# One-hots of an adjacency build, made chunk by chunk with per-partition scalars instead of in batches of eight chunks

## The chip, the cores and the metric

One core of one Trainium2 chip. The metric is the device time of one execution in microseconds (us). The kernel before takes 494.15 us, the median of three runs (493.7 to 494.18).

## The reference

One graph-transformer layer over N = 1250 nodes of width 512, with a graph of 21250 directed edges (`src`, `dst`, one weight each). The part that matters here is the graph part:

```python
m = jnp.maximum(jnp.max(weighting_gate), 0.0)
exp_e = jnp.exp(weighting_gate - m)
row_sum = jax.ops.segment_sum(exp_e, src, num_segments=n_nodes)
atten_e = exp_e / (row_sum[src] + 1e-06)
Mfeat = source_features @ Wm + bm
out0 = jax.ops.segment_sum(atten_e[:, None] * Mfeat[dst], src, num_segments=n_nodes)
out1 = jax.ops.segment_sum(atten_e[:, None] * Mfeat[src], dst, num_segments=n_nodes)
```

Around it stand a layer norm, a linear attention (`mix`) whose result is added, and at the end a mixture of eight experts on the sum.

## The kernel before

The kernel writes out, by hand, one instruction stream for each engine, with semaphores between them. The two segment sums are done as matrix products with a dense adjacency `adj` (1250 x 1250, kept as 10 row tiles of 125 nodes by 5 windows of 250 columns, so 50 buckets). `adj` is built in three steps.

First the edges are sorted into buckets of (row tile, column window), each bucket padded to whole chunks of 128 edges: NCH = 216 chunks, taken as PAIRS = 108 pairs of two. GpSimd scatters most edges into a DRAM table `slots`; the last 54 columns of edges are placed by matmuls with one-hots instead (line 702, semaphore `sort_ps`). VectorE then adds the two parts (lines 1248 and 1250) into `keys` (row and column of each edge within its tile and window) and `parts` (the edge weight as two f16 parts, WT = 2).

Second, the adjacency build. For each chunk, TensorE multiplies a weighted row one-hot (`s_hot`, 128 edges by CH = 128 rows, once for each of the two weight parts) with a column one-hot (`d_hot`, 128 edges by AW = 251 columns; the last column is 1 and gives row sums). That is four matmuls for a pair (line 739), all f16, which add into one of four PSUM banks; a one-column matmul (line 731) resets ahead of each pair. ScalarE copies two windows (502 columns) out to `adj` after each pair (line 1646, `win_ok`). The reset of pair p waits for `win_ok` of p - 2. The banks and columns to use are data: TensorE loads them into registers, the 16 of `in_at` at every pair with p % 8 = 0 and the 8 of `new_at` at every pair with p % 8 = 4 (`read_in`, `read_new`).

The one-hots come from VectorE, in 28 batches: 26 of four pairs (eight chunks), then two of two pairs. A batch of four is three instructions: `s_one`, the plain row one-hots of eight chunks (line 1264); `d_hot`, the column one-hots (line 1268); and `s_hot`, the row one-hots times both weight parts (line 1276). All are two-operand f16 instructions on a table of column numbers that stores each number twice (`col_2`), so that the two chunks of a pair lie interleaved, element by element. `d_hot` and `s_hot` are rings of DB = 4 batches. TensorE waits for `batch_ok` once for each batch, VectorE for `chunk_ps` before it overwrites a ring entry. Before its first pair TensorE runs RUN_UP = 10 matmuls that nobody reads (line 708).

Third, once all 108 copies are done (`win_ok`), VectorE sums rows (line 1287), and TensorE turns `adj` (line 751) and multiplies with it (lines 758 and on). The update, the router and the experts follow in order.

Of the kernel before, what the change touches and what calls it, by code (L numbers as in the profile page):

```python
# [11 lines left out]
F16 = mybir.dt.float16  # L12
F32R = mybir.dt.float32r
ALU = mybir.AluOpType
# [11 lines left out]
CH = 128  # L26
# [8 lines left out]
WIN = 250  # L35
NW = N // WIN
AW = WIN + 1
# [4 lines left out]
NCH = (NE + NB * (CH - 1)) // CH + 1  # L42
# [8 lines left out]
WT = 2  # L51
E_UP, E_LEAST, E_ANY = 2.0 ** 15, 2.0 ** -24, 2.0 ** 100
PB, DB = 4, 4
# [44 lines left out]
BATCHES = [(i, i + PB) for i in range(0, PAIRS - PB, PB)] + [(PAIRS - PB, PAIRS - 2), (PAIRS - 2, PAIRS)]  # L98
# [13 lines left out]
def build(nc, x, edge_src, edge_dst, edge_w, consts, halves, biases, small, fold, wqkv, wp, bvt, w1f, w2f, b2f, out):  # L112
    with ExitStack() as ctx:
# [3 lines left out]
        def sem(name):  # L117
            return ctx.enter_context(nc.semaphore(name))
# [19 lines left out]
        def half(name):  # L138
            a, w = HALVES[name]
            return hlf[:, a:a + w]  # L140
# [15 lines left out]
        def place(name, col, shape, dt=F32):  # L156
            return nc.alloc_sbuf_tensor_at(name, shape, dt, offset=base + 4 * col)
# [56 lines left out]
        keys = place("keys", 33728, [128, 2, NCH], F16)  # L214
        parts = place("parts", 33944, [128, PAIRS // PB, WT, 2 * PB], F16)
        d_hot = place("d_hot", 16064, [128, DB, PB, AW, 2], F16)
        s_one = place("s_one", 20088, [128, 2, PB, CH, 2], F16)
        s_hot = place("s_hot", 21112, [128, DB, WT, PB, CH, 2], F16)
# [106 lines left out]
        def piece(a, i):  # L325
# [45 lines left out]
        key_ok, sort_hot, sort_ps, part_ok, col_ok, one_ok, batch_ok, chunk_ps, win_ok = (  # L371
            sem("key_ok"), sem("sort_hot"), sem("sort_ps"), sem("part_ok"), sem("col_ok"), sem("one_ok"),
            sem("batch_ok"), sem("chunk_ps"), sem("win_ok"))
# [25 lines left out]

        def batch_of(pair):  # L400

            n = next(i for i, (a, b) in enumerate(BATCHES) if a <= pair < b)
            return n, pair - BATCHES[n][0]

# [121 lines left out]
        def _(pe):  # L526
# [195 lines left out]
            for p in range(PAIRS):  # L722
# [10 lines left out]
                n, q = batch_of(p)  # L733
                if p == BATCHES[n][0]:
                    pe.wait_ge(batch_ok, n + 1)
                for j in range(2):
                    at_in = pe.snap(in_at[(2 * p + j) % BATCH], min_val=512 * WB0, max_val=512 * (WB0 + WBANKS - 1) + AW)
                    for i in range(WT):
                        mm = pe.matmul(flat_banks[:, bass.ds(at_in, AW)], s_hot[:, n % DB, i, q, :, j],  # L739
                                       d_hot[:, n % DB, q, :, j], start=False, stop=(i == WT - 1), skip_group_check=True)  # L740
# [191 lines left out]
        def _(dve):  # L932
# [309 lines left out]
            for n in range(EARLY + 1, PCOLS // 2):  # L1242
                sort_late(n)
            dve.wait_ge(sort_ps, PCOLS // 2)
            dve.memset(d_hot[:, :, :, WIN, :], 1.0)
# [4 lines left out]
            dve.tensor_tensor(parts[:, :, :, :].rearrange("p n i m -> p i n m"),  # L1250
                              got_h[:, :, 2:4].rearrange("p (n m) k -> p k n m", m=2 * PB),
                              bank[0][:, 0:2 * NCH].rearrange("p (k n m) -> p k n m", k=2, m=2 * PB),
                              ALU.add).then_inc(part_ok, 1)
            dve.wait_ge(part_ok, 1)
            dve.wait_ge(col_ok, 1)
            for n, (p0, p1) in enumerate(BATCHES):
                k, r = p1 - p0, n % DB

                def of_keys(i):
                    return keys[:, i, 2 * p0:2 * p1].rearrange("p (a j) -> p a j", j=2).unsqueeze(2)  # L1260

                if n >= 2:
                    dve.wait_ge(batch_ok, n - 1)
                dve.tensor_tensor(s_one[:, n % 2, 0:k, :, :], col_2[:, 0:CH, :].unsqueeze(1).to_broadcast([128, k, CH, 2]),
                                  of_keys(0).to_broadcast([128, k, CH, 2]), ALU.is_equal).then_inc(one_ok, 1)
                if n >= DB:
                    dve.wait_ge(chunk_ps, BATCHES[n - DB][1])
                dve.tensor_tensor(d_hot[:, r, 0:k, 0:WIN, :], col_2[:, :, :].unsqueeze(1).to_broadcast([128, k, WIN, 2]),  # L1268
                                  of_keys(1).to_broadcast([128, k, WIN, 2]), ALU.is_equal)
                if n == 0:  # L1270
                    dve.wait_ge(part_ok, 2)
                dve.wait_ge(one_ok, n + 1)
                both = parts[:, p0 // PB, :, :].rearrange("p i (a j) -> p i a j", j=2)
                if k == PB:
                    shape = [128, WT, PB, CH, 2]
                    last = dve.tensor_tensor(s_hot[:, r, :, :, :, :], s_one[:, n % 2, :, :, :].unsqueeze(1).to_broadcast(shape),  # L1276
                                             both.unsqueeze(3).to_broadcast(shape), ALU.mult)
                else:
                    a = p0 % PB
                    for i in range(WT):  # L1280
                        last = dve.tensor_tensor(s_hot[:, r, i, 0:k, :, :], s_one[:, n % 2, 0:k, :, :],
                                                 both[:, i, a:a + k, :].unsqueeze(2).to_broadcast([128, k, CH, 2]), ALU.mult)
                last.then_inc(batch_ok, 1)
# [576 lines left out]
```

## Time and profile before

| | |
|---|---|
| median of 3 runs | 494.15 us (493.7 to 494.18) |
| profiled execution, its own time | 493.5 us |
| its span, from the first to the last instruction | 491.4 us |
| adjacency build, first pair's matmul to last copy | 231.5 to 312.5 us |
| VectorE busy, adjacency build, batches | 228.4 to 305.8 us |
| granted TensorE clock, mean | 0.959 |

```profile
## 2 busy tenths in 40 slices
PE   3665999999999999999777777899898957999992
DVE  6786688877786888698999998478279874455552
ACT  4577999988897123363777777554335662666550
PEclk9878999999999999999999999999999858999998
```

Each digit is one fortieth of the span, about 12.3 us, and gives the busy share in tenths. PE is TensorE's matmuls, DVE VectorE, ACT ScalarE; PEclk is the TensorE clock granted, in tenths of full. The adjacency build is the 19th to 25th digit. Start times below are in us from the start of the span, and a duration is an instruction's own, which for VectorE overlaps a little with the next one's.

### The profile page before, as it was taken

How to read it: one execution, taken by the hardware profiler on the slowest of the kernel's cores; microseconds unless marked ns; L12 is line 12 of the kernel's file. 1: busy time of each engine (PE TensorE's matmuls, PEld its weight loads, DVE VectorE, ACT ScalarE, POOL GpSimd, SP SyncE). 2: the span in 40 equal slices, each digit the busy share in tenths (PEclk: the TensorE clock that was granted, in tenths of full speed). 3: DMA queues.
4: the chain of work that ended last, by engine and by line, in shares of the span. 5: the costliest groups of instructions: out<-in, count | busy, mean ns of one | idle time of the engine just before them, and what ended most of it. 6: DMA issues, size and time to landing. Idle time of an engine off the chain costs nothing.

```text
span 491.4 us, 8811 instructions
## 1 busy us (share of the span) xinstructions
PE 424.5 (86%) x2701; PEld 343.4 (70%) x2701; DVE 366.9 (75%) x717; ACT 298.3 (61%) x845; POOL 194.8 (40%) x160
## 2 busy tenths in 40 slices
PE   3665999999999999999777777899898957999992
PEld 1454887888887788877555555799876746788881
DVE  6786688877786888698999998478279874455552
ACT  4577999988897123363777777554335662666550
POOL 0378878688887787870000000000000008254321
PEclk9878999999999999999999999999999858999998
DMA  7992000000000000005000000000006964243210
GB/s 228 284 250 49 1 3 3 1 4 2 3 3 1 2 2 3 2 3 191 2 1 2 1 2 0 3 1 0 1 1 258 412 225 128 74 120 110 68 65 16
DMA packets 15742, 31.07 MB, mean 63 GB/s; under 512 B 7652, under 2 KB 8283, under 8 KB 14675
## 3 DMA queue, kind: packets, MB, share of 16 engines
q1 hardware_dynamic: 9266, 23.21, 14.6%
q0 software_dynamic: 6432, 7.31, 7.5%
q8 instruction: 24, 0.39, 0.3%
q14 instruction: 20, 0.16, 0.1%
HBM read 24.90 MB, written 7.37 MB: 66 GB/s over the span
## 4 chain that ended last, share of the span: by engine, by line
PE 64%; ACT 14%; DVE 10%; issue 6%; DMA 3%; POOL 1%; SPq 1%; ACTq 0%; DVEq 0%; POOLq 0%
PE banks L569 25%; PE banks L739 9%; PE banks L892 7%; PE banks L758 4%; ACT adj L1646 4%; PE banks L751 2%; ACT q_sb L1580 2%; PE banks L824 2%; PE banks L650 2%; PE banks L883 2%; ACT k_sb L1580 1%; DVE chunk_1h L1214 1%; DMA x_rows<-factors 1%; ACT q_sb L1563 1%; PE banks L731 1%
## 5 line engine op out<-in xcount | busy, mean ns | idle before, releaser
L496 POOL DMA_INDIRECT slots<-record,row_i x116 | 153.7, 1325 | 40.7 <-issue 40.7
L507 POOL DMA_INDIRECT rec<-x_rows,get_i x17 | 18.7, 1098 | 190.7 <-DMA x_rows<-factors 185.8
L1646 ACT ACTIVATE adj<-banks x108 | 58.4, 588 | 27.9 <-PE banks L739 26.8
L569 PE MATMUL banks<-w_hi,xT_hi 128*125 128x512 f32 (+1 forms) x160 | 61.5, 385 | 5.7 <-DVE xT_lo L1085 5.7
L739 PE MATMUL banks<-d_hot,s_hot 128*128 128x251 f16 x432 | 60.0, 276 | 0.2
L569 PE MATMUL banks<-w_lo,xT_hi 128*125 128x512 f32 (+1 forms) x160 | 60.1, 375 | 0.0
L569 PE MATMUL banks<-w_hi,xT_lo 128*125 128x512 f32 (+1 forms) x160 | 60.0, 375 | 0.0
L569 PEld LDWEIGHTS banks<-w_hi,xT_hi 128*125 128x125 f32 x160 | 30.9, 193 | 12.0 <-issue 6.1
L739 PEld LDWEIGHTS banks<-d_hot,s_hot 128*128 128x128 f16 x432 | 33.5, 98 | 7.5 <-issue 0.7
L569 PEld LDWEIGHTS banks<-w_lo,xT_hi 128*125 128x125 f32 x160 | 30.9, 193 | 5.8
L569 PEld LDWEIGHTS banks<-w_hi,xT_lo 128*125 128x125 f32 x160 | 30.6, 191 | 6.1
L516 POOL DMA_INDIRECT out<-o_sb,out_i x17 | 17.1, 1005 | 40.9 <-DVE o_sb L1462 40.9
L1268 DVE TENSOR_TENSOR d_hot<-col,keys 128x2000 f16<-128x2000 f16 (+1 forms) x28 | 32.3, 1153 | 0.0
L731 PE MATMUL banks<-hlf 128*128 128x1 f16 x108 | 18.3, 170 | 16.1 <-ACT adj L1646 16.1
L1276 DVE TENSOR_TENSOR s_hot<-s_one,parts 128x2048 f16<-128x2048 f16 x26 | 31.6, 1215 | 0.0
L1457 DVE TENSOR_TENSOR y_sb<-banks,b_sb 128x512 f32<-128x512 f32 x17 | 11.8, 691 | 26.2 <-PE banks L569 26.2
L731 PEld LDWEIGHTS banks<-hlf 128*128 128x128 f16 x108 | 10.4, 96 | 28.9 <-issue 26.9
L1580 ACT ACTIVATE q_sb<-q_sb,hmax 125x64 f32<-125x64 f32 x80 | 26.7, 335 | 4.3 <-DVE hmax L1113 4.2
L1609 ACT ACTIVATE row_1h<-row_one,sort_f 125x128 f16<-125x128 f16 x54 | 19.7, 432 | 13.8 <-DVE row_one L1208 8.0
L1580 ACT ACTIVATE k_sb<-k_sb,hmax 125x64 f32<-125x64 f32 x80 | 26.6, 333 | 0.0
L702 PE MATMUL banks<-chunk_1h,row_1h 125*128 125x216 f16 x216 | 22.8, 258 | 3.2 <-DVE chunk_1h L1214 2.2
L1617 ACT ACTIVATE xT_hi<-banks 128x500 fp32r<-128x500 f32 x10 | 5.9, 588 | 30.6 <-PE banks L663 30.6
(297 smaller groups left out, 1083.1 us busy)
## 6 DMA issues: line engine op xcount, KB each, us to landing
w_raw<-in_w2f SPq DMA_DIRECT2D x4, 1024.0 KB, 8.1
w_raw<-in_wqkv SPq DMA_DIRECT2D x3, 1024.0 KB, 15.2
x_rows<-rec SPq DMA_DIRECT2D x10, 224.0 KB
w1a<-in_w1f SPq DMA_DIRECT2D x1, 2048.0 KB, 7.8
w1b<-in_w1f SPq DMA_DIRECT2D x1, 2048.0 KB, 16.5
b_sb<-in_b2f SPq DMA_DIRECT2D x1, 2048.0 KB, 22.9
slots<-record,row_i POOLq DMA_INDIRECT x116, 2.6
rec<-in_x SPq DMA_DIRECT2D x1, 1120.0 KB
```

The costliest lines, as they stand in the source:

```text
L496: pool.indirect_dma_start(slots, bass.IndirectOffsetOnAxis(ap=row_i[:, c:c + 1], axis=0), record[:, c, :], None).then_inc(slot_st, 16)
L569: mm = pe.matmul(dst, ab, cd, start=(i == 0), stop=(i == n - 1))
L702: mm = pe.matmul(bank[1 - v // 2][:, v % 2 * NCH:(v % 2 + 1) * NCH], row_1h[:, n % RS, v, :, j], chunk_1h[:, n % RS, :, j], start=(n == 0 ...
L731: pe.matmul(flat_banks[:, bass.ds(at_new, 1)], before, zero_col, start=True, stop=False, skip_group_check=True)
L739: mm = pe.matmul(flat_banks[:, bass.ds(at_in, AW)], s_hot[:, n % DB, i, q, :, j], d_hot[:, n % DB, q, :, j], start=False, stop=(i == WT - ...
L758: mm = pe.matmul(hid_at(w), msg[:, t, GH:MD], adjw[:, t, w, 0:WIN], start=(t == 0), stop=(t == NT - 1), skip_group_check=True)
L892: mm = pe.matmul(bank[1][:, 0:F], xsT[:, c % 2, k, :], w1_sb[k // 2][:, k % 2, bass.ds(e * F, F)], start=(k == 0), stop=(k == KD - 1))
L1268: dve.tensor_tensor(d_hot[:, r, 0:k, 0:WIN, :], col_2[:, :, :].unsqueeze(1).to_broadcast([128, k, WIN, 2]), of_keys(1).to_broadcast([128, ...
L1276: last = dve.tensor_tensor(s_hot[:, r, :, :, :, :], s_one[:, n % 2, :, :, :].unsqueeze(1).to_broadcast(shape), both.unsqueeze(3).to_broadc ...
L1580: last = act.activation(ah, ah, ACT.Exp, bias=hmax[:, i, h:h + 1], accum_out=hsum[:, i, h:h + 1])
L1609: last = act.activation(row_1h[:, n % RS, VD, :, j], row_one[:, n % 2, :, j], ACT.Copy, scale=sort_f[:, 2 * n + j:2 * n + j + 1])
L1646: act.activation(adj[:, bass.ds(w, BW2)], flat_banks[0:TP, bass.ds(out_at, BW2)], ACT.Copy).then_inc(win_ok, 1)
```

## The change

`keys` and `parts` become f32, one column for each chunk. The table `col_2`, the intermediate `s_one` and the batches are no longer used in this stage. For each chunk VectorE now issues three `tensor_scalar` instructions: one compares the table of 250 column numbers with that chunk's column key, given as a per-partition scalar, and writes `d_hot`; two compare the 128 row numbers with the row key and multiply by one weight part, both as per-partition scalars, and write one part of `s_hot` each. The two chunks of a pair lie one after the other instead of interleaved. The rings hold RING_P = 16 pairs. TensorE waits once for each pair (`hot_pair`), and VectorE waits for `chunk_ps` pair by pair from the 17th on. The matmuls, the resets, the copies and the register loads stay.

```diff
--- before.py
+++ after.py
@@ -50,7 +50,8 @@
 HB = BATCH // 2
 WT = 2
 E_UP, E_LEAST, E_ANY = 2.0 ** 15, 2.0 ** -24, 2.0 ** 100
-PB, DB = 4, 4
+RING_P = 16
+DW = AW + 1
 WB0, WBANKS, IDLE_IN, IDLE_OUT = 2, 4, 6, 7
 TRASH, SPARE = NB * AW, 4
 BW2 = 2 * AW
@@ -95,7 +96,6 @@
 
 
 PAIRS = NCH // 2
-BATCHES = [(i, i + PB) for i in range(0, PAIRS - PB, PB)] + [(PAIRS - PB, PAIRS - 2), (PAIRS - 2, PAIRS)]
 LOTS = [(i * LC, min(i * LC + LC, EC)) for i in range(NL)]
 MARKED = (3, 6, 8, 9)
 
@@ -211,11 +211,11 @@
         row_1h = place("row_1h", 16584, [TP, RS, VT, CH, 2], F16)
         got = place("got", 32216, [128, NCH, RW])
         got_h = got[:, :, :].bitcast(F16)
-        keys = place("keys", 33728, [128, 2, NCH], F16)
-        parts = place("parts", 33944, [128, PAIRS // PB, WT, 2 * PB], F16)
-        d_hot = place("d_hot", 16064, [128, DB, PB, AW, 2], F16)
-        s_one = place("s_one", 20088, [128, 2, PB, CH, 2], F16)
-        s_hot = place("s_hot", 21112, [128, DB, WT, PB, CH, 2], F16)
+        keys = place("keys", 33728, [128, 2, NCH])
+        parts = place("parts", 34160, [128, WT, NCH])
+        d_hot = place("d_hot", 16064, [128, RING_P, 2, DW], F16)
+        s_hot = place("s_hot", 21112, [128, RING_P, WT, 2, CH], F16)
+
 
 
         hidc = place("hidc", 26064, [128, 2, WIN])
@@ -368,9 +368,9 @@
             sem("num_ps"), sem("num_used"), sem("ao_ok"), sem("aoT_ps"), sem("aoT_ok"), sem("mix_ps"), sem("mix_ok"))
 
         sort_one, sort_act = sem("sort_one"), sem("sort_act")
-        key_ok, sort_hot, sort_ps, part_ok, col_ok, one_ok, batch_ok, chunk_ps, win_ok = (
-            sem("key_ok"), sem("sort_hot"), sem("sort_ps"), sem("part_ok"), sem("col_ok"), sem("one_ok"),
-            sem("batch_ok"), sem("chunk_ps"), sem("win_ok"))
+        key_ok, sort_hot, sort_ps, part_ok, col_ok, hot_pair, chunk_ps, win_ok = (
+            sem("key_ok"), sem("sort_hot"), sem("sort_ps"), sem("part_ok"), sem("col_ok"),
+            sem("hot_pair"), sem("chunk_ps"), sem("win_ok"))
         rinv_ok, in_ok, in_ps, turn_ps, turn_a, turn_v, out_split = (
             sem("rinv_ok"), sem("in_ok"), sem("in_ps"), sem("turn_ps"), sem("turn_a"), sem("turn_v"),
             sem("out_split"))
@@ -396,11 +396,6 @@
 
             for a, b in ((0, 112), (112, TP)):
                 eng.dma_start(dst(a, b), srcs(a, b)).then_inc(s, 16)
-
-        def batch_of(pair):
-
-            n = next(i for i, (a, b) in enumerate(BATCHES) if a <= pair < b)
-            return n, pair - BATCHES[n][0]
 
         def ctx_copies(copy, h):
 
@@ -730,14 +725,12 @@
                     pe.wait_ge(win_ok, p - 2)
                 pe.matmul(flat_banks[:, bass.ds(at_new, 1)], before, zero_col, start=True, stop=False,
                           skip_group_check=True)
-                n, q = batch_of(p)
-                if p == BATCHES[n][0]:
-                    pe.wait_ge(batch_ok, n + 1)
+                pe.wait_ge(hot_pair, p + 1)
                 for j in range(2):
                     at_in = pe.snap(in_at[(2 * p + j) % BATCH], min_val=512 * WB0, max_val=512 * (WB0 + WBANKS - 1) + AW)
                     for i in range(WT):
-                        mm = pe.matmul(flat_banks[:, bass.ds(at_in, AW)], s_hot[:, n % DB, i, q, :, j],
-                                       d_hot[:, n % DB, q, :, j], start=False, stop=(i == WT - 1), skip_group_check=True)
+                        mm = pe.matmul(flat_banks[:, bass.ds(at_in, AW)], s_hot[:, p % RING_P, i, j, :],
+                                       d_hot[:, p % RING_P, j, 0:AW], start=False, stop=(i == WT - 1), skip_group_check=True)
                 mm.then_inc(chunk_ps, 1)
 
 
@@ -1242,45 +1235,25 @@
             for n in range(EARLY + 1, PCOLS // 2):
                 sort_late(n)
             dve.wait_ge(sort_ps, PCOLS // 2)
-            dve.memset(d_hot[:, :, :, WIN, :], 1.0)
+            dve.memset(d_hot[:, :, :, WIN:DW], 1.0)
 
             dve.wait_ge(ld_got, 16)
             dve.tensor_tensor(keys[:, :, :], got_h[:, :, 0:2].rearrange("p c k -> p k c"),
                               bank[1][:, 0:2 * NCH].rearrange("p (k c) -> p k c", k=2), ALU.add).then_inc(part_ok, 1)
-            dve.tensor_tensor(parts[:, :, :, :].rearrange("p n i m -> p i n m"),
-                              got_h[:, :, 2:4].rearrange("p (n m) k -> p k n m", m=2 * PB),
-                              bank[0][:, 0:2 * NCH].rearrange("p (k n m) -> p k n m", k=2, m=2 * PB),
-                              ALU.add).then_inc(part_ok, 1)
-            dve.wait_ge(part_ok, 1)
-            dve.wait_ge(col_ok, 1)
-            for n, (p0, p1) in enumerate(BATCHES):
-                k, r = p1 - p0, n % DB
-
-                def of_keys(i):
-                    return keys[:, i, 2 * p0:2 * p1].rearrange("p (a j) -> p a j", j=2).unsqueeze(2)
-
-                if n >= 2:
-                    dve.wait_ge(batch_ok, n - 1)
-                dve.tensor_tensor(s_one[:, n % 2, 0:k, :, :], col_2[:, 0:CH, :].unsqueeze(1).to_broadcast([128, k, CH, 2]),
-                                  of_keys(0).to_broadcast([128, k, CH, 2]), ALU.is_equal).then_inc(one_ok, 1)
-                if n >= DB:
-                    dve.wait_ge(chunk_ps, BATCHES[n - DB][1])
-                dve.tensor_tensor(d_hot[:, r, 0:k, 0:WIN, :], col_2[:, :, :].unsqueeze(1).to_broadcast([128, k, WIN, 2]),
-                                  of_keys(1).to_broadcast([128, k, WIN, 2]), ALU.is_equal)
-                if n == 0:
-                    dve.wait_ge(part_ok, 2)
-                dve.wait_ge(one_ok, n + 1)
-                both = parts[:, p0 // PB, :, :].rearrange("p i (a j) -> p i a j", j=2)
-                if k == PB:
-                    shape = [128, WT, PB, CH, 2]
-                    last = dve.tensor_tensor(s_hot[:, r, :, :, :, :], s_one[:, n % 2, :, :, :].unsqueeze(1).to_broadcast(shape),
-                                             both.unsqueeze(3).to_broadcast(shape), ALU.mult)
-                else:
-                    a = p0 % PB
+            dve.tensor_tensor(parts[:, :, :], got_h[:, :, 2:4].rearrange("p c k -> p k c"),
+                              bank[0][:, 0:2 * NCH].rearrange("p (k c) -> p k c", k=2), ALU.add).then_inc(part_ok, 1)
+            dve.wait_ge(part_ok, 2)
+            places = half("cols")
+            for p in range(PAIRS):
+                if p >= RING_P:
+                    dve.wait_ge(chunk_ps, p - RING_P + 1)
+                for j in range(2):
+                    c = 2 * p + j
+                    dve.tensor_scalar(d_hot[:, p % RING_P, j, 0:WIN], places, keys[:, 1, c:c + 1], None, ALU.is_equal)
                     for i in range(WT):
-                        last = dve.tensor_tensor(s_hot[:, r, i, 0:k, :, :], s_one[:, n % 2, 0:k, :, :],
-                                                 both[:, i, a:a + k, :].unsqueeze(2).to_broadcast([128, k, CH, 2]), ALU.mult)
-                last.then_inc(batch_ok, 1)
+                        last = dve.tensor_scalar(s_hot[:, p % RING_P, i, j, :], places[:, 0:CH], keys[:, 0, c:c + 1],
+                                                 parts[:, i, c:c + 1], ALU.is_equal, ALU.mult)
+                last.then_inc(hot_pair, 1)
 
 
             dve.wait_ge(win_ok, PAIRS)
```

## Rows read from the trace of the kernel before

**Rows 1.** The chain that ended last, 225 to 314 us: its share by line

```profile
by line: PE banks L739 51.6%; ACT adj L1646 22.8%; issue 9.1%; PE banks L731 5.9%; PE banks L708 4.8%; ACTq L1646 1.6%; PE banks L751 1.5%; PE banks L702 1.1%; DVE chunk_1h L1214 0.8%; DVE row_1h L1212 0.6%; PE banks L758 0.3%; DVE row_one 
```

**Rows 2.** Busy time by stretch: us, each engine's busy time (instructions), clock, DMA

```profile
core 0: us, PE busy (x) PEld busy (x) DVE busy (x) ACT busy (x) POOL busy (x), PEclk, DMA share, GB/s
...
271.00:281.00 10.00, 7.84 (x70) 5.45 (x68) 10.00 (x12) 6.95 (x13) 0.00 (x0) 1.00 0.00 0
301.00:312.00 11.00, 9.08 (x79) 6.12 (x76) 4.76 (x10) 8.19 (x16) 0.00 (x0) 1.00 0.01 1
...
409.00:413.20 4.20, 1.99 (x11) 1.29 (x10) 1.49 (x1) 2.11 (x3) 3.29 (x4) 0.99 0.45 131
413.20:416.60 3.40, 3.40 (x11) 2.63 (x10) 0.08 (x1) 0.00 (x0) 2.51 (x3) 0.51 0.70 187
```

**Rows 3.** Order of time, 268 to 277 us: start, duration, engine, line, idle before

```profile
268.31 0.68 DVE L1264 TENSOR_TENSOR s_one<-col,keys 128x1024 f16<-128x1024 f16 x1
...
268.91 1.19 DVE L1268 TENSOR_TENSOR d_hot<-col,keys 128x2000 f16<-128x2000 f16 x1
...
270.02 1.22 DVE L1276 TENSOR_TENSOR s_hot<-s_one,parts 128x2048 f16<-128x2048 f16 x1
...
270.38 0.17 PE L731 MATMUL banks<-hlf 128*128 128x1 f16 x1 [0.37 <-ACT adj L1646]
...
271.16 0.68 DVE L1264 TENSOR_TENSOR s_one<-col,keys 128x1024 f16<-128x1024 f16 x1
...
273.65 0.17 PE L731 MATMUL banks<-hlf 128*128 128x1 f16 x1 [0.91 <-ACT adj L1646]
...
276.38 0.17 PE L731 MATMUL banks<-hlf 128*128 128x1 f16 x1 [0.36 <-ACT adj L1646]
```

**Rows 4.** Who waited for whom, 228 to 313 us

```profile
ACT adj L1646 <- PE banks L739: 26.8, 28, 6.1
PE banks L731 <- ACT adj L1646: 16.1, 26, 1.0
```

**Rows 5.** Order of time around the start and the end of the build

```profile
227.20 4.39 PE L708 MATMUL banks<-cst 128*128 128x250 f32 x20
...
228.44 0.68 DVE L1264 TENSOR_TENSOR s_one<-col,keys 128x1024 f16<-128x1024 f16 x1
...
305.01 0.75 DVE L1281 TENSOR_TENSOR s_hot<-s_one,parts 128x512 f16<-128x512 f16 x2
...
311.12 0.63 PE L739 MATMUL banks<-d_hot,s_hot 128*128 128x251 f16 x4
312.51 0.24 DVE L1287 TENSOR_REDUCE rs<-adj 125x10 f32<-125x50 f32 x1 [6.75 <-ACT adj L1646]
```

**Rows 6.** Groups on VectorE by shape: busy us, mean ns of one

```profile
L1462 DVE SCALAR_TENSOR_TENSOR o_sb<-y_sb,rec 128x512 f32<-128x512 f32 x17 | 12.8, 752 | 0.6
...
L1457 DVE TENSOR_TENSOR y_sb<-banks,b_sb 128x512 f32<-128x512 f32 x17 | 11.8, 691 | 26.2 <-PE banks L569 26.2
```

**Rows 7.** Order of time on VectorE, instructions with and without per-partition scalars

```profile
3.77 0.25 DVE L943 TENSOR_SCALAR s_hi<-src_i 125x170 int32<-125x170 int32 x1 [3.77 <-DMA dst_i<-in_edge_dst]
3.93 0.24 DVE L944 TENSOR_SCALAR d_hi<-dst_i 125x170 int32<-125x170 int32 x1
...
73.22 0.14 DVE L1073 TENSOR_SCALAR of_c<-of_b 125x1 f32<-125x1 f32 x1
73.28 0.20 DVE L1074 TENSOR_SCALAR of_c<-of_b,cst 125x1 f32<-125x1 f32 x1
...
358.95 0.60 DVE L1343 TENSOR_SCALAR hid<-comb,mv,rstd 125x128 f32<-125x128 f32 x2
...
362.39 0.61 DVE L1323 TENSOR_SCALAR comb<-banks,rinv 125x128 f32<-125x128 f32 x2 [1.64 <-PE banks L794]
```

**Rows 8.** Lines 1323 and 1343: durations min/median/max, ns

```profile
L1323 DVE TENSOR_SCALAR comb<-banks,rinv x10: 339/342/351, 350.8 to 376.2; 125x128 f32<-125x128 f32 x10
...
L1343 DVE TENSOR_SCALAR hid<-comb,mv,rstd x10: 339/344/348, 353.2 to 379.6; 125x128 f32<-125x128 f32 x10
```


## Prediction

> **What bounds the kernel now.** I read the chain that ended last first, cut to the adjacency build and its edges. The reader is to see that VectorE is all but absent from it: 51.6% lies on the four matmuls of a pair (line 739), 22.8% on ScalarE's copies (line 1646), 9.1% on issue [rows 1]. Then busy time by stretch: in the middle of the build VectorE is busy 10.00 us of 10, TensorE 7.84, ScalarE 6.95, and after the batches end VectorE falls to 4.76 of 11 [rows 2]. So there are two loops of nearly the same pace. The order of time gives both. VectorE starts a batch of four pairs at 268.31 and the next at 271.16: 2.85 us, 0.71 us a pair. TensorE starts the reset of a group at 270.38, the next at 273.65, the third at 276.38: 6.00 us for eight pairs, 0.75 us a pair [rows 3]. In the list of waits nobody waits for VectorE: ScalarE waits 26.8 us for line 739 and TensorE 16.1 us for the copies [rows 4]. TensorE's loop (matmuls, copies, register loads) sets the pace, and VectorE runs ahead: its last batch is done at 305.76, while the last pair's matmuls start at 311.12 and the row sum that opens the next stage at 312.51, 6.75 us after VectorE went idle [rows 5]. VectorE has 0.04 us a pair to spare, and 5.4 us at the end. Whatever makes its pair dearer than 0.75 us moves the end of the stage.
>
> **Part 1: what goes.** Per four pairs, `s_one` takes 0.60 us from its start to the next instruction's, `d_hot` 1.11 and `s_hot` 1.14 [rows 3]. These give the law for a two-operand f16 instruction: 1024 elements 0.60 us, 2048 elements 1.14 us, so 0.53 ns an element, two elements per 1.05 ns, and about 0.06 us fixed. Instructions of this size pay the fixed part three times in four pairs. It hardly counts.
>
> **Part 2: what comes.** Per pair, two `tensor_scalar` of 250 elements with one per-partition scalar and four of 128 elements with two, six instructions in place of 0.75. In all 648 instructions in place of 86. Each has three prices: the fixed part, a charge for the scalar, and the elements by a rate.
>
> The fixed part without such a scalar: line 943, 170 int32 elements with a constant, starts 0.16 us before line 944 [rows 7]. With two elements per 1.05 ns that is 0.09 + 0.07. I take 0.065 us.
>
> The charge for the scalar: line 1074 has one element and a per-partition scalar and takes 0.20 us, line 1073 the same with a constant 0.14 [rows 7]. Line 1462, 512 elements with one such scalar, takes 752 ns where line 1457 without takes 691 [rows 6]. Both give 0.06 us.
>
> Whether it hides when such instructions follow each other: line 1323 (PSUM source, 128 elements, one scalar) does two in 0.61 us, one taking 342 ns, so they start 0.27 us apart; 0.065 + 0.134 + 0.06 = 0.26 [rows 7, 8]. It doesn't hide. Line 1343 (SBUF source, two scalars, a subtraction and a multiplication, the very form of the new `s_hot`, in f32) does two in 0.60 us, one taking 344 ns: 0.26 us apart [rows 7, 8]. That row can be read in two ways. A: one charge whatever the number of scalars, and one element per 1.05 ns (0.065 + 0.134 + 0.06 = 0.26). B: a charge for each scalar, and two elements per tick (0.065 + 0.067 + 0.12 = 0.25).
>
> For f16 no row has a `tensor_scalar`. Under A the engine keeps one operand path, and f16 packing gives two elements a tick as in rows 3: `d_hot` 0.065 + 0.131 + 0.06 = 0.256, `s_hot` 0.065 + 0.067 + 0.06 = 0.192, a pair 0.512 + 0.768 = 1.28 us. Under B f16 doubles f32's rate to four a tick: `d_hot` 0.191, `s_hot` 0.219, a pair 0.382 + 0.876 = 1.26 us. The two come out alike, so I need not choose. I take 1.28, the end that lies with the slightly dearer measured spacing. The bounds from the nearest rows: below, no charge and four a tick, 2 x 0.131 + 4 x 0.099 = 0.66 us; above, f16 treated as line 1343 under A, one element a tick, 2 x 0.387 + 4 x 0.259 = 1.81 us.
>
> The Trainium skill, "VectorE: DVE Perf Modes", section on the TRN2 errata, puts a VectorE instruction on SBUF at 58 cycles of 0.96 GHz plus the elements over the mode's factor, and its tier table lets `tensor_scalar` on 16-bit data run at 4x. By it the pair would be an estimated 0.63 us, cheaper than now. The same section warns that the fixed cost is paid per instruction and advises 512 elements or more, which speaks against this change; and its formula has no term for the scalar, which rows 6 and 7 show at 0.06 us.
>
> **Part 3: the waits.** TensorE waits for each pair instead of each fourth; behind that wait stand its four matmuls, and behind those ScalarE's copy. The reset is ahead of it. Price: a wait that is met costs nothing that rows 3 show (between zero and 0.03 us a pair if VectorE is ahead); if VectorE is late it is VectorE's time, counted below. VectorE's new wait for `chunk_ps` looks 16 pairs back, as the ring of four batches did, and is met long before. The f32 sum for `keys` and `parts` is as large as now; VectorE's loop starts after both instead of after the first, at about 228.6 instead of 228.44 [rows 5], 0.1 to 0.2 us. That TensorE could have its first pair at 230 is worth nothing: its idle matmuls of line 708 run from 227.20 to 231.59 [rows 5]. Contiguous operands for the matmuls: zero; they run at 2.4 GHz by their columns already (clock 1.00 [rows 2]). The extra column of a ring row and the memset of 64 instead of 32 elements: below 0.05 us.
>
> **The sum.** VectorE: 228.6 + 108 x 1.28 = 366.8. Then the last pair: 0.1 us for the end of the last write and the signal, and from the start of its matmuls to the row sum 312.51 - 311.12 = 1.39 us [rows 5]. The row sum starts at 368.3 instead of 312.51: +55.8 us. What follows it doesn't depend on anything that runs beside the build, so it shifts as it is.
>
> **The clock.** TensorE would be busy 7.84 us of 13.3 pairs, 0.59 us a pair [rows 2], in 1.28 us: 46%. The stretch 409 to 413.2 has 1.99 of 4.20 us, 47%, and after it the clock reads 0.51, the 1.2 GHz level, for 3.4 us of dense work [rows 2]. So I expect a fall during the build. At half clock a pair is at most 1.17 us and with today's gaps (2.16 us in 13.3 pairs) at most 1.33, so at worst 0.05 us a pair more than VectorE's (+5 us); I expect none, since busy time counts a pipeline's fill that doesn't double. The next stage would start low: half of 3.4 us lost, 1.7, and 0.5 for the last pair: 2.2 us. Bounds 0 and 7.
>
> 493.5 (the profiled execution: span 491.4 and 2.1 around it) + 55.8 + 2.2 = 551.5. The median of the runs is 0.65 above the profiled one: 552.2.
>
> **Rivals.**
>
> *The scalars stop every fast mode.* Line 1343 under A, and f16 no better: 1.81 us a pair, 195.5 us, the row sum at 425.6, +113.1. With the clock's 2.2: 609. For it: one row, read one way. Against: rows 3 show f16 packing on the same engine.
>
> *One charge and four a tick.* 2 x 0.191 + 4 x 0.159 = 1.02 us, 109.9 us, +27.5: 524. It needs line 1343 to have been slowed by something that f16 escapes.
>
> *The charge hides in a long run, at two a tick.* 2 x 0.196 + 4 x 0.132 = 0.92 us, 99.4 us, +17: 513.
>
> *No charge at all, four a tick: the other side.* 0.66 us a pair is below TensorE's 0.75, so VectorE is hidden as now, and TensorE's loop of 6.00 us for eight pairs sets the end: 81 us from 231.5, what it takes now. 494, between 492.5 (waits of the first groups gone) and 496 (a wait for each pair). It decides below 0.75 us a pair. The skill's formula above is this rival. Lines 1323 and 1343, back to back and still 0.26 apart, speak against it.
>
> **How the numbers follow.** The forecast (1.24 to 1.34 us a pair, 546 to 562) 58%; every fast mode lost 13%; one charge at four a tick 12%; the charge hidden at two a tick 6%; no charge 9%; elsewhere between 2%. The point is 552. The range takes in the forecast, the dear rival and the case at 524, 83%: 522 to 612. A measurement of this kernel can tell 0.2%, 1 us, from no change. Of the 9% I give 3 to faster, 4 to same, 2 to slower; all else is slower: 0.93.
>
> **What would show it.** In the profile after: VectorE busy without a gap from 228.6 to about 367, `d_hot` durations near 0.34 us under A or 0.28 under B, `s_hot` near 0.28 or 0.30, with starts 0.06 to 0.08 us closer than durations; the idle time before line 739's matmuls put down to VectorE; no idle time before the row sum beyond some 1.5 us; the clock at 0.5 in the build and for some 3 us after. The prediction is wrong if the pair's starts are under 1.2 us apart, if the clock stays at 1.00 (then 2.2 us less), or if TensorE's pace at half clock exceeds VectorE's.

## The result and the profile after

The changed kernel takes 550.85 us (550.45 to 551.78, four runs) against 493.92 (492.47 to 494.18) before: a ratio of 1.116, 95% interval 1.113 to 1.119. Predicted were 552.0. The profiled execution has a span of 548.4 us, 57.0 more than before.

From the page after: the engines' busy times and the forty slices.

```profile
PE 469.9 (86%) x2701; PEld 360.1 (66%) x2701; DVE 428.1 (78%) x1279; ACT 303.5 (55%) x845; POOL 192.4 (35%) x160
...
PE   4485999999989999868888887879998885899992
...
PEclk9977999999999999965555555558999995999998
```

VectorE's busy time rose by 61 us (366.9 before), TensorE's by 45 (424.5 before) with the same 2701 matmuls. The clock reads 0.5 to 0.6 for ten slices in the middle, where it was full before. Who waited for whom in the build, and the chain's share by line from 225 to 371 us:

```profile
PE banks L732 <- DVE s_hot L1254: 19.0, 67, 0.7
...
by line: DVE s_hot L1254 65.6%; DVE d_hot L1252 29.3%; PE banks L744 1.5%; PE banks L732 0.7%; PE banks L697 0.7%; DVE chunk_1h L1207 0.5%; ACT adj L1619 0.4%; DVE row_1h L1205 0.4%; issue 0.4%; DVE parts L1243 0.4%; DVE keys L1241 0.3%; DV
```

Before, nobody waited for VectorE and the chain ran over TensorE and ScalarE [rows 1, 4]. Now two VectorE lines carry 95% of it. Order of time at the start and the end of the build, and the first use of line 1296 (line 1323 before), which I take as the mark behind the turning stage, in which TensorE turns `adj` and multiplies with it:

```profile
230.33 0.28 DVE L1252 TENSOR_SCALAR d_hot<-hlf,keys 128x250 f16<-128x250 f16 x1
230.53 0.53 DVE L1254 TENSOR_SCALAR s_hot<-hlf,keys,parts 128x128 f16<-128x128 f16 x2
230.97 0.28 DVE L1252 TENSOR_SCALAR d_hot<-hlf,keys 128x250 f16<-128x250 f16 x1
...
231.29 0.59 PE L732 MATMUL banks<-d_hot,s_hot 128*128 128x251 f16 x4
...
366.96 1.02 PE L732 MATMUL banks<-d_hot,s_hot 128*128 128x251 f16 x4 [0.26 <-DVE s_hot L1254]
...
368.74 0.24 DVE L1260 TENSOR_REDUCE rs<-adj 125x10 f32<-125x50 f32 x1 [1.92 <-ACT adj L1619]
...
368.85 2.43 PE L744 MATMUL banks<-cst,adj 125*125 125x125 f32 x10 [0.87 <-ACT adj L1619]
...
409.84 0.35 DVE L1296 TENSOR_SCALAR comb<-banks,rinv 125x128 f32<-125x128 f32 x1 [5.72 <-PE banks L787]
```

The same mark before:

```profile
350.77 0.35 DVE L1323 TENSOR_SCALAR comb<-banks,rinv 125x128 f32<-125x128 f32 x1 [5.72 <-PE banks L794]
```

`d_hot` starts 0.195 us before the next instruction; two `s_hot` together take 0.445, so 0.22 each; the next chunk starts 0.64 us later, a pair 1.28. The row sum starts at 368.74 instead of 312.51 [rows 5]: +56.2 us. TensorE's first pair still starts only after its idle matmuls, at 231.29, and the first turn of a tile takes 2.43 us.

Busy time by stretch, columns as in [rows 2]:

```profile
231.00:237.70 6.70, 4.05 (x35) 2.70 (x34) 6.70 (x33) 3.43 (x6) 0.00 (x0) 1.00 0.23 98
...
271.00:281.00 10.00, 8.39 (x40) 4.57 (x40) 10.00 (x48) 4.48 (x8) 0.00 (x0) 0.50 0.00 1
...
471.90:475.30 3.40, 2.53 (x14) 1.83 (x12) 0.42 (x1) 1.27 (x3) 2.50 (x3) 1.00 0.70 185
```

At full clock TensorE is busy 4.05 us of 6.70 (and 1.85 of the last 3.70), then the clock falls at 237.7 and stays at 0.50 until 374.3, in the turning stage. The busy time it then shows, 8.39 of 10, is the same four matmuls and reset a pair at 1.2 GHz: 1.07 us a pair instead of 0.59.

### The profile page after: what moved, and what is told of

It is laid out like the page before. It is cut to its first block, busy times and chain, and to the rows that moved or that the text cites. A ratio compares the mean times of both kernels' runs of the same rounds, so it can differ in the third digit from the quotient of the medians.

```text
span 548.4 us, 9371 instructions
## 1 busy us (share of the span) xinstructions
PE 469.9 (86%) x2701; PEld 360.1 (66%) x2701; DVE 428.1 (78%) x1279; ACT 303.5 (55%) x845; POOL 192.4 (35%) x160
## 4 chain that ended last, share of the span: by engine, by line
PE 49%; DVE 35%; ACT 9%; issue 4%; POOL 1%; SPq 0%; DMA 0%; DVEq 0%; ACTq 0%; POOLq 0%
PE banks L564 22%; DVE s_hot L1254 17%; DVE d_hot L1252 8%; PE banks L885 6%; PE banks L751 4%; PE banks L744 2%; ACT q_sb L1553 2%; PE banks L645 1%; PE banks L868 1%; PE banks L876 1%; ACT k_sb L1553 1%; DVE chunk_1h L1207 1%; PE banks L532 1%; ACT q_sb L1536 1%; DVE stat L1331 1%
## 5 line engine op out<-in xcount | busy, mean ns | idle before, releaser
L491 POOL DMA_INDIRECT slots<-record,row_i x116 | 151.5, 1306 | 40.7 <-issue 40.7
L732 PE MATMUL banks<-d_hot,s_hot 128*128 128x251 f16 x432 | 105.8, 401 | 20.3 <-DVE s_hot L1254 19.0
L1254 DVE TENSOR_SCALAR s_hot<-hlf,keys,parts 128x128 f16<-128x128 f16 x432 | 112.2, 297 | 0.0
L1619 ACT ACTIVATE adj<-banks x108 | 63.5, 589 | 79.2 <-PE banks L732 79.1
L732 PEld LDWEIGHTS banks<-d_hot,s_hot 128*128 128x128 f16 x432 | 45.6, 128 | 53.4 <-issue 40.0
L1252 DVE TENSOR_SCALAR d_hot<-hlf,keys 128x250 f16<-128x250 f16 x216 | 58.8, 272 | 0.0
L726 PEld LDWEIGHTS banks<-hlf 128*128 128x128 f16 x108 | 14.7, 136 | 22.8 <-issue 18.1
L726 PE MATMUL banks<-hlf 128*128 128x1 f16 x108 | 21.6, 200 | 6.4 <-issue 6.2
L751 PE MATMUL banks<-adj,msg 125*128 125x250 f32 x100 | 24.6, 396 | 0.0
```

The source lines that it names most:

```text
L491: pool.indirect_dma_start(slots, bass.IndirectOffsetOnAxis(ap=row_i[:, c:c + 1], axis=0), record[:, c, :], None).then_inc(slot_st, 16)
L726: pe.matmul(flat_banks[:, bass.ds(at_new, 1)], before, zero_col, start=True, stop=False, skip_group_check=True)
L732: mm = pe.matmul(flat_banks[:, bass.ds(at_in, AW)], s_hot[:, p % RING_P, i, j, :], d_hot[:, p % RING_P, j, 0:AW], start=False, stop=(i == ...
L751: mm = pe.matmul(hid_at(w), msg[:, t, GH:MD], adjw[:, t, w, 0:WIN], start=(t == 0), stop=(t == NT - 1), skip_group_check=True)
L1252: dve.tensor_scalar(d_hot[:, p % RING_P, j, 0:WIN], places, keys[:, 1, c:c + 1], None, ALU.is_equal)
L1254: last = dve.tensor_scalar(s_hot[:, p % RING_P, i, j, :], places[:, 0:CH], keys[:, 0, c:c + 1], parts[:, i, c:c + 1], ALU.is_equal, ALU.mult)
```

## Experiments

The theory on the pair's price: a fixed part of 0.065 us, 0.06 us for each per-partition scalar, not hidden in a long run of such instructions, and f16 elements at four per 1.05 ns. The rivals: one charge an instruction, a floor for short instructions, a charge for f32 scalars beside an f16 stream, and a slow rate. The first four runs build on the changed kernel. The diffs are shortened: `...` stands for what is left out, and small edits that only make room for them (a copy of the keys in f32, the layout of a ring) are told in words. Where one run is given and no range, the program ran once.

**One scalar instead of two.**

```diff
-                        ... keys[:, 0, c:c + 1], parts[:, i, c:c + 1], ALU.is_equal, ALU.mult)
+                        ... keys[:, 0, c:c + 1], 1.0, ALU.is_equal, ALU.mult)
```

> The changed kernel with the constant 1.0 in place of the weight part as second scalar of s_hot (it leaves the edge weights out of adj). Theory (each per-partition scalar costs 0.06 us, not hidden): s_hot spacing 0.225 to 0.165 us, d_hot unchanged at 0.195, a pair 1.28 to 1.04 us, the build 26 us shorter, about 525 us. Rival (one charge for an instruction, whatever the number of scalars; the rest of the 0.225 is the second ALU operation): no change, 551 us.

Measured 523.42 us (one run). Order of time on VectorE:

```profile
260.17 0.42 DVE L1254 TENSOR_SCALAR s_hot<-hlf,keys 128x128 f16<-128x128 f16 x2
260.50 0.29 DVE L1252 TENSOR_SCALAR d_hot<-hlf,keys 128x250 f16<-128x250 f16 x1
260.69 0.41 DVE L1254 TENSOR_SCALAR s_hot<-hlf,keys 128x128 f16<-128x128 f16 x2
```

Two `s_hot` take 0.33 us from the first's start to the next `d_hot`, 0.165 each, and `d_hot` 0.19. The pair is 1.04 us. The second ALU operation is still there, the second scalar isn't: the charge is for each scalar. This row also sets the rate: with one scalar each, 250 columns cost 0.19 and 128 cost 0.165, some 0.03 us for 122 columns, which is four per 1.05 ns (0.032) and not two (0.064). (`s_hot` still has one ALU operation more than `d_hot`; were that dear, the columns would be cheaper still.)

**No per-partition scalar.**

```diff
-  dve.tensor_scalar(d_hot[...], places, keys[:, 1, c:c + 1], None, ALU.is_equal)
+  dve.tensor_scalar(d_hot[...], places, float(c), None, ALU.is_equal)
-  dve.tensor_scalar(s_hot[...], places[:, 0:CH], keys[:, 0, c:c + 1], parts[:, i, c:c + 1], ALU.is_equal, ALU.mult)
+  dve.tensor_scalar(s_hot[...], places[:, 0:CH], float(c % CH), 1.0, ALU.is_equal, ALU.mult)
```

> The changed kernel with constants in place of all per-partition scalars (it leaves keys and weights out, so adj holds other numbers). Theory (fixed part 0.065 us, four elements per 1.05 ns): d_hot spacing 0.131 us, s_hot 0.099, a pair 0.66 us, below TensorE's loop of 0.75 us, so the time is again the kernel before's, 493 to 496 us. Rival (short f16 instructions have a floor of about 0.19 us each whatever their scalars): a pair 1.15 us or more, 535 us or more.

Measured 495.79 us. Order of time on VectorE, and its row sum:

```profile
260.14 0.29 DVE L1254 TENSOR_SCALAR s_hot<-hlf 128x128 f16<-128x128 f16 x2
260.35 0.22 DVE L1252 TENSOR_SCALAR d_hot<-hlf 128x250 f16<-128x250 f16 x1
260.48 0.29 DVE L1254 TENSOR_SCALAR s_hot<-hlf 128x128 f16<-128x128 f16 x2
...
312.88 0.24 DVE L1260 TENSOR_REDUCE rs<-adj 125x10 f32<-125x50 f32 x1 [10.22 <-ACT adj L1619]
```

0.105 and 0.13 us, a chunk 0.34, a pair 0.68: below TensorE's 0.75, and the row sum is back at 312.88. The same 648 instructions, the same waits for each pair and the same layout move the row sum by 0.4 us once VectorE is under TensorE's pace. The loss of 56 us there is in the scalars: 0.30 of the 0.64 us a chunk.

**f16 scalars.** `keys` and `parts` are kept as F16.

> The changed kernel with keys and parts kept as f16, so that the per-partition scalars are f16 instead of f32. Theory (the charge is a fixed latency of fetching the scalar, and f32 scalars don't hold the fast mode back): spacing 0.195 and 0.225 us as in the changed kernel, 551 us. Rival (the charge is the f32 scalar beside an f16 stream): the spacing falls to some 0.13 and 0.10 us, towards 494 us.

Measured 551.08 us.

```profile
260.05 0.29 DVE L1252 TENSOR_SCALAR d_hot<-hlf,keys 128x250 f16<-128x250 f16 x1
260.25 0.54 DVE L1254 TENSOR_SCALAR s_hot<-hlf,keys,parts 128x128 f16<-128x128 f16 x2
260.69 0.29 DVE L1252 TENSOR_SCALAR d_hot<-hlf,keys 128x250 f16<-128x250 f16 x1
```

0.20 and 0.22 us, as in the changed kernel. The scalar's type doesn't matter. Durations of `s_hot` read 0.31 here where the changed kernel showed 0.30, at the same spacing: between profiles only the spacing may be compared.

**TensorE kept busy.** The clock theory: its fall comes from TensorE's own idle time in the build.

```diff
                     pe.matmul(flat_banks[:, bass.ds(at_new, 1)], before, zero_col, ...)
+                if p >= 4:
+                    for _ in range(3):
+                        pe.matmul(bank[IDLE_IN][:, 0:WIN], before, half("cols"), start=True, stop=True)
                 pe.wait_ge(hot_pair, p + 1)
```

> The changed kernel, plus three matmuls of 250 columns that nobody reads, ahead of TensorE's wait for each pair from the fifth on. Theory (the clock fell in the build because TensorE waits for VectorE's one-hots there; cost 3.2 us: 0.4 in the last pair, 2.8 in the next stage): clock 1.00 through the build, VectorE's pair unchanged at 1.28 us, row sum at about 368.3, first use of line 1296 about 3.2 us earlier, 547.6 us in all. Rival (the clock follows something else, such as VectorE's use of SBUF): the clock falls all the same, seven matmuls a pair at half clock take about 1.6 us and TensorE becomes the bound, some 580 us.

Measured 550.46 us (547.66 to 552.07, four runs), ratio to before 1.117 (1.110 to 1.124). Order of time at the end of the build, the first use of line 1299 (1296 in the changed kernel), and the stretch 251 to 301:

```profile
365.74 0.60 PE L735 MATMUL banks<-d_hot,s_hot 128*128 128x251 f16 x4 [0.33 <-DVE s_hot L1257]
...
367.10 0.24 DVE L1263 TENSOR_REDUCE rs<-adj 125x10 f32<-125x50 f32 x1 [1.50 <-ACT adj L1622]
...
405.37 0.61 DVE L1299 TENSOR_SCALAR comb<-banks,rinv 125x128 f32<-125x128 f32 x2 [5.72 <-PE banks L790]
...
251.00:301.00 50.00, 35.88 (x310) 23.75 (x309) 50.00 (x236) 23.05 (x40) 0.00 (x0) 1.00 0.01 2
```

The clock stays at 1.00, with TensorE busy 35.88 us of 50, and VectorE gets through as many instructions (236) in these 50 us as in the changed kernel. From the last pair's matmuls to the row sum it takes 1.36 us, in the changed kernel 1.78; from the row sum to line 1299 38.27, there 41.10, and before 38.26. So the fall costs 0.4 and 2.8 us as the theory said, and filling TensorE's idle time takes it away. The total doesn't show it beyond the spread: what comes after that line takes 140.9 us here and 138.6 in the changed kernel's profile. The clock there reads 0.78, 0.50 and 0.53 in the three stretches of 10 us that begin 30 us after that line, and 1.00, 0.50 and 0.65 in the changed kernel; that this is the whole of the 2.3 us is not shown. That part of the expectation, 547.6 us, came out only in the fastest run.

The next two do one part of the change alone, on the kernel before.

**`d_hot` alone by chunk.** The ring keeps its four batches, now with the two chunks of a pair one after the other; the keys are copied to f32 once.

```diff
-  dve.tensor_tensor(d_hot[:, r, 0:k, 0:WIN, :], col_2..., of_keys(1)..., ALU.is_equal)
+  for c in range(2 * p0, 2 * p1):
+      dve.tensor_scalar(d_hot[:, r, c // 2 - p0, c % 2, 0:WIN], half("cols"), keys_f[:, c:c + 1], None, ALU.is_equal)
```

> The kernel before with the d_hot part of the change alone: 216 instructions of 250 columns with one f32 per-partition scalar, in a ring of four batches as before; s_one and s_hot stay in batches. Theory: a batch 0.60 + 8 x 0.195 + 1.14 = 3.30 us instead of 2.85, 0.825 us a pair, just above TensorE's 0.75, so VectorE bounds the build: row sum at about 320.2 instead of 312.5, 501 us. Rival (single instructions of this size cost more among large ones, or less): the d_hot spacing is not 0.195 us.

Measured 503.26 us.

```profile
264.62 0.69 DVE L1267 TENSOR_TENSOR s_one<-col,keys 128x1024 f16<-128x1024 f16 x1
265.22 1.65 DVE L1273 TENSOR_SCALAR d_hot<-hlf,keys_f 128x250 f16<-128x250 f16 x8
266.78 1.23 DVE L1280 TENSOR_TENSOR s_hot<-s_one,parts 128x2048 f16<-128x2048 f16 x1
267.91 0.70 DVE L1267 TENSOR_TENSOR s_one<-col,keys 128x1024 f16<-128x1024 f16 x1
...
320.01 0.24 DVE L1291 TENSOR_REDUCE rs<-adj 125x10 f32<-125x50 f32 x1 [2.28 <-ACT adj L1650]
```

A batch is 3.29 us, eight `d_hot` 1.56 of it, 0.195 each also between large instructions, 0.82 us a pair. The row sum is at 320.01, 7.5 us later than before and as expected: VectorE passes TensorE's 0.75 and becomes the bound. The total is 2.3 us above the 501 expected; those lie behind the row sum (181.2 us to the end of the span, 178.9 before), where nothing was changed.

**`s_hot` alone by chunk.** `s_one` goes, the row keys are copied to f32 once, and `parts` is f32.

```diff
-  s_one: dve.tensor_tensor(...)   s_hot: dve.tensor_tensor(...)
+  for c in range(2 * p0, 2 * p1):
+      for i in range(WT):
+          dve.tensor_scalar(s_hot[:, r, i, c // 2 - p0, c % 2, :], half("cols")[:, 0:CH], keys_f[:, c:c + 1],
+                            parts[:, i, c:c + 1], ALU.is_equal, ALU.mult)
```

> The kernel before with the s_hot part of the change alone: 432 instructions of 128 columns with two f32 per-partition scalars in place of s_one and s_hot; d_hot stays in batches. Theory: a batch 1.11 + 16 x 0.225 = 4.71 us, 1.18 us a pair, row sum at about 358, 540 us and perhaps 2 to 3 more for the clock. The two parts then add up: 0.11 + 0.47 us a pair over 0.71 gives the 1.28 of the change. Rival (they interact): they don't add up.

Measured 536.81 us.

```profile
264.47 1.25 DVE L1265 TENSOR_TENSOR d_hot<-col,keys 128x2000 f16<-128x2000 f16 x1
265.58 3.71 DVE L1269 TENSOR_SCALAR s_hot<-hlf,keys_f,parts 128x128 f16<-128x128 f16 x16
269.14 1.26 DVE L1265 TENSOR_TENSOR d_hot<-col,keys 128x2000 f16<-128x2000 f16 x1
...
355.67 0.24 DVE L1275 TENSOR_REDUCE rs<-adj 125x10 f32<-125x50 f32 x1 [2.07 <-ACT adj L1634]
```

Sixteen `s_hot` take 3.56 us, 0.2225 each; a batch 4.67, 1.17 us a pair. Over the 0.71 of before the two parts add 0.11 and 0.46: 1.28, the changed kernel's pair. They don't interact. The 540 expected was 3 too much: 0.0025 us for each of 432 instructions is 1.1, and this stage began 1.4 us earlier in its profile (first `d_hot` at 227.06, first `s_one` before at 228.44). TensorE's clock went back and forth here (0.76 on the mean from 251 to 301 us) and stood at 1.00 again by the row sum, so the 2 to 3 us for the clock didn't come: from row sum to the mark it took 38.27 us.

The last three runs, on the kernel before, ask whether TensorE's 0.75 us a pair, the bound of the kernel before, can be lowered by its register loads.

```diff
-                if p % HB == 0: read_in(2 * p)             # 16 registers
-                if p % HB == HB // 2: read_new(p)          # 8
+                if p % G == 0: read_in(2 * p); read_new(p)  # 2 * G and G; G = 2 (b_spread), 4 (b_spread4)
```

> The kernel before with TensorE's register loads spread: four in_at and two new_at at every second pair, instead of 16 and 8 at every eighth. Theory (TensorE's loop of 6.00 us for eight pairs holds two bursts of loads that its queue can't cover; VectorE could give 5.70): the loop falls to 5.7 to 5.8 us, the build ends 3 to 4 us earlier, 490 us. Rival (a load costs by the instruction, not by the register): eight loads in place of two for eight pairs, the loop 6.3 us or more, 498 us.

> As the run before it, with eight in_at and four new_at at every fourth pair, four loads for eight pairs instead of two. Theory (cost by the register, bursts halved): the two groups of four pairs take the same time, 2.9 to 3.0 us each, 492 to 494 us. Rival (cost by the instruction): 495 us or more.

Measured 517.81 us (513.96 to 519.98, ratio 1.048, 1.043 to 1.054) and 496.78 us (494.21 to 497.93, ratio 1.008, 1.005 to 1.011). No gain either way. TensorE's resets that open eight pairs, with G = 4:

```profile
261.94 0.17 PE L727 MATMUL banks<-hlf 128*128 128x1 f16 x1 [0.76 <-ACT adj L1642]
...
268.21 0.17 PE L727 MATMUL banks<-hlf 128*128 128x1 f16 x1 [0.76 <-ACT adj L1642]
```

That is 6.27 us for eight pairs instead of 6.00 [rows 3] with two more loads and the same number of registers. I read this as a load that costs by the instruction, some 0.13 us, and tried fewer: 24 and 12 registers, each loaded at every 12th pair.

> The kernel before with 24 and 12 registers, each loaded at every 12th pair, half a period apart, instead of 16 and 8 at every eighth. The runs with more loads took 6.27 us (four loads) and about 7.8 us (eight loads) for eight pairs against 6.00 with two. Theory (a load costs by the instruction, 0.13 us or more, and TensorE's loop sets the kernel before's pace): 1.33 loads for eight pairs give 5.8 to 5.95 us, at most VectorE's 5.70, and a build 1 to 2.5 us shorter: 491 to 492.5 us. Rival (the longer load makes a longer burst that the queue can't cover): 6.0 us or more, no gain.

Measured 516.54 us (515.91 to 518.21, ratio 1.044, 1.041 to 1.047). TensorE's resets that open a half period:

```profile
263.18 0.18 PE L731 MATMUL banks<-hlf 128*128 128x1 f16 x1 [2.65 <-issue]
...
269.10 0.18 PE L731 MATMUL banks<-hlf 128*128 128x1 f16 x1 [0.44 <-issue]
```

TensorE stood still for 2.65 us ahead of one reset and 0.44 ahead of the next. Which load stands ahead of which, and what each takes, the loads' own records say: first those of the kernel before (16 and 8 registers), then of G = 2 (4 and 2), of G = 4 (8 and 4) and of this run (24 and 12, and the one ahead of 263.18), with the shortest, median and longest duration in ns:

```profile
L715 PEldq TENSOR_LOAD <-at_i x14: 588/1103/1119, 228.5 to 308.5; - x14
L719 PEldq TENSOR_LOAD <-at_i x14: 589/592/784, 227.7 to 305.8; - x14
...
L714 PEldq TENSOR_LOAD <-at_i x54: 328/332/536, 227.7 to 334.8; - x54
L717 PEldq TENSOR_LOAD <-at_i x54: 533/537/543, 228.3 to 335.2; - x54
...
L714 PEldq TENSOR_LOAD <-at_i x27: 587/592/786, 226.7 to 311.1; - x27
L717 PEldq TENSOR_LOAD <-at_i x27: 327/331/351, 227.6 to 311.8; - x27
...
L715 PEldq TENSOR_LOAD <-at_i x9: 1614/1616/1629, 231.0 to 324.7; - x9
L719 PEldq TENSOR_LOAD <-at_i x10: 1046/2880/2887, 229.9 to 330.2; - x10
L719 PEldq TENSOR_LOAD <-at_i x1: 2880/2880/2880, 260.0 to 260.0; - x1
```

`PEldq` marks work of TensorE's sequencer. The long standstill is behind the load of 12 registers, which runs from 260.0 to 262.88, and not behind that of 24. And a load costs by the register: 4, 8, 16 and 24 take 0.33, 0.59, 1.10 and 1.62 us, which is 0.064 us for each register and some 0.08 fixed. Two kinds of load are dearer, 0.54 us for 2 registers and 2.88 for 12, some 0.23 us for each register. The dear ones start at a column of `at_i`, or hold a number of registers, that is no multiple of four (the 12 are loaded from columns 6, 18, 30 and so on; from column 0, as the first load of the run, they took 1.05). In all the cheap ones both are multiples of four. No run separates the two conditions, and none tests another cause. By these prices the loads of eight pairs take 1.70 us before, 1.85 with G = 4 and 3.48 with G = 2, and those of 12 pairs 4.50 here against 2.54 before: the versions come out in this order. So both my theory, that shorter bursts would gain, and the 0.13 us by the instruction fell: that figure was a difference between two loops and not a load's price. The rival (a longer burst) named the right outcome for a reason that the records don't show, since the 24 registers cost what their number says. A version with 12 registers loaded from multiples of four is untested; no version that I ran beats the kernel before.

## Why the prediction was right, step by step

**The bound.** Right, and the threshold too. The two loops run at 0.71 and 0.75 us a pair, and what passes 0.75 on VectorE moves the end: at 0.68 the row sum stood at 312.88, at 0.82 at 320.01, at 1.17 at 355.67, at 1.28 at 368.74. One reading beneath it was off: the 16.1 us that TensorE waits for the copies [rows 4] go with its register loads. From 262 to 301 us each of these waits stands ahead of the first reset behind a register load; one such load of 16 registers runs from 272.3 to 273.4, and the reset follows at 273.65. So TensorE's loop of 6.00 us is long by its loads, 1.27 us of idle time in eight pairs [rows 3]. The forecast didn't need this.

**The price of the instructions.** Right in the sum: 1.28 us a pair was forecast and measured. But I forecast it from two readings of line 1343 that give nearly the same sum (1.28 and 1.26), and took the dearer. That this one hit the number is luck: its terms are wrong. Reading B is the true one: 0.191 and 0.219 us were its terms, 0.195 and 0.2225 the measured ones; A's 0.256 and 0.192 were both wrong by as much as they cancel. Had the change had three `d_hot` to one `s_hot`, choosing A would have been off by 0.15 us in 0.81. My remark that I need not choose holds for this mix of instructions alone. The rival in which the scalars stop every fast mode (609 us) falls with A: `d_hot` at the slow rate would have been 0.387.

**The charge for a scalar.** 0.06 us each, shown by the run with one scalar (0.2225 to 0.165) and the one with none (to 0.105, and `d_hot` from 0.195 to 0.13). The Trainium skill, "VectorE: DVE Perf Modes", section on the TRN2 errata, has 58 cycles plus the elements over the mode's factor; the run without scalars agrees nearly (0.125 and 0.094 us by an estimate from it, 0.13 and 0.105 measured), the changed kernel doesn't (0.195 and 0.2225), since the formula has no term for the scalar. Its advice to use 512 elements or more isn't what decided here: without scalars the same instructions of 128 and 250 elements give a pair in 0.68 us, less than the 0.71 of the large ones before.

**The waits and the start.** Priced at nothing, and rightly: the loop began at 228.40 (228.6 forecast). From its first start to the row sum it took 140.3 us against 139.7 in the sum. Of the 0.6 left, 0.4 is the slow last pair, which the sum had under the clock.

**The clock.** The mechanism was right, its size a little small: 0.5 + 1.7 forecast, 0.4 + 2.8 measured. I had forecast TensorE busy 46% of the time before the fall; read were 4.05 us of 6.70 (60%) from 231 to 237.7, where the first pairs had gathered behind the idle matmuls, and 1.85 of 3.70 (50%) in the part from 234 on. The level stayed low for 5.6 us after the row sum, to 374.3, where I had taken 3.4 us. That length isn't a constant: in the run with f16 scalars, the same stage at the same pace, the clock was full again some 3 us after the row sum, and the stage took 39.67 us (369.01 to 408.68), 1.4 and not 2.8 above the 38.27 at full clock. The worry that TensorE at half clock would be slower than VectorE was for nothing: TensorE kept up at half clock, and VectorE's spacing shows no stall.

**What the sum didn't have.** "It shifts as it is" was wrong by 2.0 us, on the lucky side, which hid the 1.1 us missing in the clock's term. From the first use of line 1323 to the end of the span before takes 140.6 us, after 138.6. The clock has a part in it that I can't size. Before, it is at 0.51 from 413.2 to 416.6 with TensorE busy all of it [rows 2], and the matching stretch after, 471.9 to 475.3, is at 1.00; but another dense stretch after, 464.4 to 467, is at 0.52 where the matching one before, 406.4 to 409, is at 1.00. Adding up in the profiled executions: +56.2 (with 0.4 of the clock) + 2.8 - 2.0 = +57.0, as the spans differ. Where the clock falls in the expert stage differs between profiles, and runs of the kernel before alone spread from 489.8 to 496.8 us over all comparisons, so a term of 1 or 2 us behind the build can't be called right or wrong by the total.

## What to carry to other kernels

When loops of two engines share a stage, read each one's period from the order of time and note the gap; the cheaper engine's slack, here 0.04 us a pair, decides what an edit on it may cost before the end moves. Price a small instruction as fixed part, charge for each per-partition scalar and elements by rate, each from its own row, and check that the sum fits a row where such instructions stand back to back. Replacing few large two-operand instructions by many of 128 to 250 elements with scalars loses even when the elements run twice as fast, since of 0.64 us a chunk some 0.30 are charges for five scalars, 0.20 three fixed parts, and only 0.13 elements.

## What the runs showed that I had not expected

TensorE's register loads have a price that can be read from their own records: 0.064 us for each register and some 0.08 for the load, and 0.23 us for each register in the loads of 2, and of 12 from columns 6, 18 and so on. With G = 2 the loop took some 7.8 us for eight pairs instead of 6.0, partly at the lower clock (0.86 on the mean from 251 to 301 us). The idle time ahead of the resets, read without these records, had led me to a wrong rule.

The clock doesn't always settle. At 1.04 us a pair (one scalar less) and at 1.17 (`s_hot` alone) it went back and forth between both levels, 0.78 and 0.76 on the mean from 251 to 301 us, where it was 0.50 at 1.28 us a pair and 1.00 at 0.82.
